# Cross attention and mixture of experts: the last unit's sums, residuals, router rows and first keys in another order

## The reference, cut to what matters

```python
# attention, on the layer-normed x; keys and values are both ctx
qn, kn = l2norm(q), l2norm(k)                     # over the 64 channels of a head
sm = softmax(5.0 * einsum('bhdq,bhdk->bhqk', qn, kn), axis=-1)
x = x + einsum('bhqk,bhdk->bhdq', sm, v)
# experts, on the layer-normed new x: 2048 tokens, 4 experts, capacity 512 each
logits = tokens @ Wg + bg                         # 2048 x 4
top_vals, top_idx = top_k(logits, 2);  probs = softmax of these two
for i in range(4):
    p, idx = top_k(where(i in top_idx, probs[:, i], -inf), 512)
    out[idx] += gelu(tokens[idx] @ W1[i]) @ W2[i] * p
x = x + out
```

## Time and profile before

| | us |
|---|---|
| three runs | 598.73, 602.92, 599.44 |
| median | 599.44 |
| the profiled execution, its time | 601.62 |
| its span, first to last instruction | 599.8 |

### The profile page before, as it was taken

One profiled execution on the slowest core, in us unless ns is written; L12 is line 12 of the kernel. 1 busy time (PEld: TensorE's weight loads), 2 busy tenths in 40 slices (PEclk: granted clock), 3 DMA queues, 4 the chain that ended last, 5 costly groups with the idle time before them and its releaser, 6 DMA issues.

```text
span 599.8 us, 8893 instructions
## 1 busy us (share of the span) xinstructions
PE 569.5 (95%) x2936; PEld 405.8 (68%) x2936; DVE 341.8 (57%) x682; ACT 292.6 (49%) x451; POOL 183.0 (31%) x146
## 2 busy tenths in 40 slices
PE   8999999999998558999999999999999999999994
PEld 4445555545544325888888888888888888888883
DVE  5779999999978683534345434346434346334212
ACT  3989888788884323333234343234343243343310
POOL 8456565565633425000401500401500401500002
PEclk9999999999997859999999999999999999999998
DMA  5524433433223134322622532622632612632001
GB/s 156 194 73 124 143 106 110 141 109 104 90 89 113 65 105 140 120 91 71 184 98 89 198 135 70 203 77 87 209 123 76 203 70 94 198 128 71 0 1 70
DMA packets 49005, 67.91 MB, mean 113 GB/s; under 512 B 10961, under 2 KB 27473, under 8 KB 48977
## 3 DMA queue, kind: packets, MB, share of 16 engines
q1 hardware_dynamic: 45136, 54.97, 28.1%
q0 software_dynamic: 3840, 12.59, 6.2%
HBM read 54.77 MB, written 12.64 MB: 112 GB/s over the span
## 4 chain that ended last, share of the span: by engine, by line
PE 86%; DVE 6%; issue 3%; POOL 2%; ACT 1%; DMA 1%; DVEq 0%; POOLq 0%; ACTq 0%
PE two L1532 29%; PE four L1562 10%; PE four L1561 10%; PE four L1559 10%; PE two L1355 9%; PE four L1345 7%; PE two L1370 2%; PE bank_t L1390 2%; PE bank_m L1317 1%; PE bank_t L1324 1%; PE four L1397 1%; DVE junk L1118 1%; PE bank_t L1382 1%; PE bank_m L1332 1%; DMA x_got<-x2n_dram,idx_all 1%
## 5 line engine op out<-in xcount | busy, mean ns | idle before, releaser
L816 ACT ACTIVATE h_f<-two 128x512 f32<-128x512 f32 x64 | 38.3, 598 | 224.2 <-PE two L1532 224.2
L1285 DVE TENSOR_TENSOR h_lo<-h_f,h_hi 128x512 fp32r<-128x512 f32 x64 | 44.1, 689 | 120.2 <-ACT h_hi L817 120.2
L1532 PE MATMUL two<-xt_hi,w_hi 128*128 (+1 forms) x256 | 101.3, 396 | 0.7 <-ACT xt_hi L805 0.7
L1532 PE MATMUL two<-xt_hi,w_lo 128*128 (+1 forms) x256 | 99.9, 390 | 0.0
L1562 PE MATMUL four<-w_hi,h_lo 128*128 128x512 f32 x256 | 99.6, 389 | 0.0
L1559 PE MATMUL four<-w_hi,h_hi 128*128 128x512 f32 x256 | 99.6, 389 | 0.0
L1561 PE MATMUL four<-w_lo,h_hi 128*128 128x512 f32 x256 | 99.6, 389 | 0.0
L1532 PE MATMUL two<-xt_lo,w_hi 128*128 (+1 forms) x256 | 99.2, 389 | 0.0
L706 ACT ACTIVATE prob<-four,rnorm 128x512 f32<-128x512 f32 x128 | 77.9, 705 | 18.2 <-POOL rnorm L518 15.0
L1255 DVE TENSOR_TENSOR w_lo<-raw,w_hi 128x2048 fp32r<-128x2048 f32 x30 | 68.7, 2291 | 23.3 <-ACT w_hi L739 23.3
L518 POOL TENSOR_TENSOR rnorm<-ss_max,power 128x8 f32<-128x8 f32 x32 | 59.2, 1851 | 43.0 <-DVE ss_max L869 28.0
(11 more groups left out here) (187 smaller groups left out, 759.2 us busy)
## 6 DMA issues: line engine op xcount, KB each, us to landing
raw<-in_L_ffn_W SPq DMA_DIRECT2D x64, 512.0 KB, 4.3
x_all<-in_x SPq DMA_DIRECT2D x16, 256.0 KB, 2.7
c_sb<-in_ctx SPq DMA_DIRECT2D x16, 256.0 KB, 3.1
out<-x_all SPq DMA_DIRECT2D x16, 256.0 KB, 2.3
x2n_dram<-x2n SPq DMA_DIRECT2D x16, 256.0 KB, 3.0
p_inv<-inv_dram SPq DMA_DIRECT2D x30, 128.0 KB, 2.8
few<-p_sum SPq DMA_DIRECT2D x60, 2.0 KB, 1.8
cst<-in_consts SPq DMA_DIRECT2D x1, 423.5 KB, 4.9
```

What stands on the lines that cost most here:

```text
L1285: nc.vector.tensor_tensor(h_lo[m % 2][:, :], h_f[m % 2][:, :], h_hi[m % 2][:, :].bitcast(F32), ALU.subtract).then_inc(h_split, 1)
L1532: return nc.tensor.matmul(z[:, :], w_part[c][:, w], x_k, start=start, stop=stop)
```

## The change

In the last unit VectorE makes half sums 0 first. TensorE's sums are done in two parts, each as soon as its half sums are there (`last_sums`), ahead of the weighted values, and the router rows of unit 12 go behind the weighted values. The residual of unit 14 moves from GpSimd to VectorE, behind `invert_sums`. The router rows of 14 go to `bank_m` as before, those of 15 to a tile of their own in SBUF (`x2n_last`), so that the transposes of 14 and 15 can both stand ahead of their products. The first keys move from the middle of unit 15 to behind `normalize_x2` of 15; the first count of round 0 goes behind the last keys. TensorE transposes the first keys behind all router products; the idle products are spread otherwise (12, 3, 2, 2 in place of 6, 3, 3, 10).

```diff
-            def residual(u):                       # on GpSimd
...
-            residual((UNITS // 2 - 1, 0))
             finish((UNITS // 2 - 1, 0))
             finish((UNITS // 2 - 1, 1))
             pool.wait_ge(x2n_done, UNITS)
             for q in range(2):
                 first_low(0, q)
-            pool.wait_ge(key_done, 2)
+            pool.wait_ge(late_keys, 1)
...
             take_x2t((UNITS // 2 - 2, 1))          # ScalarE
+            take_x2t((UNITS // 2 - 1, 0), bank_m)
+            take_x2t((UNITS // 2 - 1, 1), rows=x2n_last)
             act.wait_ge(key_set, 1)
             nc.scalar.activation(key_w[:, 0:EARLY, :, :], key[:, 0:EARLY, :].unsqueeze(3)
                                  .broadcast_to([P, EARLY, E, WAYS]), ACT.Copy).then_inc(key_done, 1)
-            take_x2t((UNITS // 2 - 1, 0), bank_m)
-            take_x2t((UNITS // 2 - 1, 1))
...
-                if behind > 2:                     # VectorE, unit
+                if behind > 2 and ahead:
                     normalize_x2(before(before(before(u))), behind > 4)
-                if not ahead:
-                    residual(before(before(u)))
-                    statistics_x2(before(before(u)))
...
                 for h in range(2):
                     half_sums(u, 0, h, behind > 0)
+                if not ahead:
+                    normalize_x2(before(before(before(u))), True)
+                    residual(before(before(u)))
                 if behind:
                     invert_few(before(u))
...
-                if not ahead:
-                    normalize_x2(before(before(u)), True)
                 for h in range(2):
                     half_sums(u, 1, h, behind > 0)
-                if not ahead:
-                    dve.wait_ge(logit_done, EARLY)
-                    keys_of(0, EARLY)
-                if behind > 2:
+                if behind > 2 and ahead:
                     take_logits(before(before(before(u))))
-                if behind > 1 and ahead:
-                    residual(before(before(u)))
+                if behind > 1:
+                    if ahead:
+                        residual(before(before(u)))
                     statistics_x2(before(before(u)))
...
             invert_sums(end)                       # VectorE, tail
+            residual(before(end))
+            residual(end, 1)
+            normalize_x2(before(before(end)), True)
+            take_logits(before(before(before(end))))
             statistics_x2(before(end))
-            residual(end, 1)
+            statistics_x2(end)
             normalize_x2(before(end), True)
             take_logits(before(before(end)))
-            statistics_x2(end)
             normalize_x2(end, True)
+            dve.wait_ge(logit_done, EARLY)
+            keys_of(0, EARLY)
             take_logits(before(end), bank_m)
+            take_logits(end)
             early = EARLY * P
+            dve.wait_ge(logit_done, UNITS)
+            keys_of(EARLY, UNITS)
+            dve.wait_ge(key_set, 2)
+            nc.vector.tensor_copy(key_w[:, EARLY:, :, :], ...).then_inc(late_keys, 1)
             dve.wait_ge(key_t, 1)
             dve.wait_ge(thr_done, 1)
             link(nc.vector.tensor_scalar(junk[:, 0:early - SIGNS], ...))
             dve.wait_ge(signs_done, 1)
             put(nc.vector.scalar_tensor_tensor(rest0[:, :], count0[:, :], -2.0, excess[:, :], ALU.mult, ALU.add))
-            take_logits(end)
-            dve.wait_ge(logit_done, UNITS)
-            keys_of(EARLY, UNITS)
-            dve.wait_ge(key_set, 2)
-            nc.vector.tensor_copy(key_w[:, EARLY:, :, :], ...).then_inc(key_done, 1)
...
+            def last_sums(u, n):                   # TensorE
+
+                for h in range(2):
+                    pe.wait_ge(halves_done[h], 2 * number(u) + n + 1)
+                pe.wait_ge(sum_taken, number(u))
+                for h in range(2):
+                    last = nc.tensor.matmul(o_ps[1][DH * h:DH * (h + 1), :], cst[:, C_ONES:C_ONES + DH],
+                                            half_sum[h][n][:, :], start=(n == 0), stop=(n == 1))
+                if n:
+                    last.then_inc(sums_ready, 1)
...
-                if behind > 2:                     # TensorE, unit
-                    router_logits(before(before(before(u))))
-                if not ahead:
-                    sums(u, behind, ahead)
-                weighted_values(u, 2)
-                weighted_values(u, 3)
-                if ahead:
-                    sums(u, behind, ahead)
+                    if behind > 2:
+                        router_logits(before(before(before(u))))
+                    weighted_values(u, 2)
+                    weighted_values(u, 3)
+                    sums(u, behind)
+                else:
+                    last_sums(u, 0)
+                    last_sums(u, 1)
+                    weighted_values(u, 2)
+                    weighted_values(u, 3)
+                    router_logits(before(before(before(u))))
...
+            idle_products(12)                      # TensorE, tail
             pe.wait_ge(logit_done, UNITS - 3)
             transpose_x2(before(before(end)))
+            idle_products(3)
             router_logits(before(before(end)))
-            pe.wait_ge(exp_done, TT * UNITS)
-            transpose_keys(0, EARLY, 1)
-            idle_products(6)
             transpose_x2(before(end), bank_m)
-            idle_products(3)
-            router_logits(before(end), bank_m)
             pe.wait_ge(logit_done, UNITS - 2)
             transpose_x2(end)
-            idle_products(3)
-            router_logits(end)
-            idle_products(10)
-            transpose_keys(EARLY, UNITS, 2)
+            router_logits(before(end), bank_m)
+            router_logits(end, rows=x2n_last)
+            idle_products(2)
+            pe.wait_ge(exp_done, TT * UNITS)
+            transpose_keys(0, EARLY, key_done)
+            idle_products(2)
+            transpose_keys(EARLY, UNITS, late_keys)
```

More of the change, by code:

```diff
@@ L314, in xattn_moe_kernel @@
         key_done = sem("key_done")
+        late_keys = sem("late_keys")
         key_t = sem("key_t")
@@ L545, in key_remainders @@
                 pool.wait_ge(k_split, n + 1)
-            def residual(u):
[L549 to L556, removed]
             def finish(u):
@@ L726, in take_sums, with take_x2t @@
                 nc.scalar.activation(p_sum[:, :], o_ps[1][:, :], ACT.Copy).then_inc(sum_taken, 1)
-            def take_x2t(u, bank=bank_t):
+            def take_x2t(u, bank=bank_t, rows=x2n_t):
                 act.wait_ge(x2t_ready, number(u) + 1)
-                nc.scalar.activation(x2n_t[:, :, :], bank[:, :].rearrange("p (k t) -> p k t", k=KD),
+                nc.scalar.activation(rows[:, :, :], bank[:, :].rearrange("p (k t) -> p k t", k=KD),
                                      ACT.Copy).then_inc(x2t_taken, 1)
@@ L1084, in _ @@
             invert_sums(end)
+            residual(before(end))
+            residual(end, 1)
+            normalize_x2(before(before(end)), True)
+            take_logits(before(before(before(end))))
             statistics_x2(before(end))
-            residual(end, 1)
+            statistics_x2(end)
             normalize_x2(before(end), True)
             take_logits(before(before(end)))
-            statistics_x2(end)
             normalize_x2(end, True)
+            dve.wait_ge(logit_done, EARLY)
+            keys_of(0, EARLY)
             take_logits(before(end), bank_m)
+            take_logits(end)
             early = EARLY * P
+            dve.wait_ge(logit_done, UNITS)
+            keys_of(EARLY, UNITS)
+            dve.wait_ge(key_set, 2)
+            nc.vector.tensor_copy(key_w[:, EARLY:, :, :], key[:, EARLY:, :].unsqueeze(3)
+                                  .broadcast_to([P, UNITS - EARLY, E, WAYS])).then_inc(late_keys, 1)
             dve.wait_ge(key_t, 1)
@@ L1357, in weighted_values, with sums @@
                 last.then_inc(pv_done, 1)
-            def sums(u, behind, ahead):
+            def sums(u, behind):
                 for h in range(2):
@@ L1366, in sums @@
                     for h in range(2):
-                        if ahead:
-                            row = QUAD * (2 * n + h)
-                            last = nc.tensor.matmul(o_ps[1][row:row + QUAD, :], cst[:, C_ONES:C_ONES + QUAD],
-                                                    half_sum[h][n][:, :], start=True, stop=True,
-                                                    tile_position=(0, row))
-                        else:
-                            last = nc.tensor.matmul(o_ps[1][DH * h:DH * (h + 1), :], cst[:, C_ONES:C_ONES + DH],
-                                                    half_sum[h][n][:, :], start=(n == 0), stop=(n == 1))
-                last.then_inc(sums_ready, 1)
+                        row = QUAD * (2 * n + h)
+                        last = nc.tensor.matmul(o_ps[1][row:row + QUAD, :], cst[:, C_ONES:C_ONES + QUAD],
```

(11 more changed lines are left out.)

4 lines of the change are left out of this document (1 added, 3 removed).

## The result

The changed kernel takes 602.54 us (median of 20 runs, 602.14 to 603.64), the kernel before 599.27 us (median of 20). The ratio is 1.0052, 95% interval 1.0042 to 1.0063: slower by 3.1 us, half a percent. Single executions far outside the rest (one of 1449.97 us among these 20 of the kernel before) are left out of all ratios. That is within 1%, as forecast, but above the range that was given (597.2 to 600.5) and on the other side of no change.

The account below looks back on a forecast made before the run. TensorE's expert stage fills most of the span; only 177 to 204 us can move. 2.2 us gained in unit 15, 1.4 lost to the moved residual, with newly exposed first keys: net 0.65 off median 599.44, 598.8 us, range 597.2 to 600.5.

Parts of the forecast that it names:

- What bounds the kernel: Whole kernel: only 177 to 204 us, 27 us or 4.5% of the span, can move; the rounds behind shift whole.
- Unit 15: Unit 15: earlier half sums and split sums let VectorE's inversion start at about 184.2, not 186.39; 2.2 us gained.
- The tail on VectorE: VectorE behind the inversion: the residual moved there takes 1.4 of the 2.2 us gained; `normalize_x2` of 15 ends at 194.7.
- T: The end of `normalize_x2` of 15 on VectorE: forecast 194.7 us, before 195.49.
- D: Length from the start of unit 14's sums to the start of the second part of round 0's count.
- From T to the rounds: Behind `normalize_x2` of 15: keys, transposes and count; the last-keys path alone gives 3.1 us, the whole 0.65.
- The first keys' way: Ahead of the rounds: ScalarE's copy, twelve transposes, signs, four transposes, no longer hidden; second part of count starts at 203.3.
- The clock: TensorE's tail: half clock when the twelve key transposes begin, returning during them or the idle products behind.
- the clock holds: Rival, chance 0.20: full clock through the key transposes, rounds begin 1.4 to 1.9 us earlier, 597.7 us.
- The base of the sum: Final sum: 0.65 us off the profiled span 599.8, then the same step off the runs' median 599.44, giving 598.8.
- slower: Rival, chance 0.08: twelve idle products at half clock delay the rows and logits of 13; 601.8 us.

Follow-up runs that it names:

- the second profile: The changed kernel, unaltered, timed and profiled again beside the kernel before: 602.8 us, ratio 1.0051; the profiled execution's own time was 602.32.
- GpSimd behind the last keys: Changed kernel with GpSimd's first two parts of `w_lo` waiting until the last keys are copied: 600.89 us, ratio 1.0020 to the kernel before.

## Why the prediction was wrong, step by step

**What bounds the kernel.** Right: only 177 to 204 us changed, and what follows shifted as a whole.

**Unit 15.** The sum put the inversion at 184.2, 8.3 us behind the start of unit 14's sums; it was 8.15 in three of the five profiles with the changed order of unit 15 and no keys in it (9.5 and 9.2 in the other two, the changed kernel's first and the one with the residual on GpSimd, where the last small transfer took 3.1 and 2.8 us to land in place of 1.8). The size was right, its reason was not: the 2.2 us were booked to the half sums and sums. The sums alone give nothing, since before the first keys ended on VectorE at 186.33, just as the sums did (183.73 + 2.63 = 186.36). Only with the keys moved away as well does the inversion move, and they have to be made somewhere.

**The tail on VectorE.** T was put 18.8 us behind that zero and was 18.3 in the second profile. The residual moved to VectorE was booked as 1.4 us lost of the gain. Left on GpSimd, it makes VectorE wait 2.3 us, so the move gains about 1 us in D. The step looked at the queue that got the work and priced at nothing the wait for the engine that lost it.

**From T to the rounds, the step that failed first.** "VectorE meanwhile makes the first keys, some 2.75 us: they end at T + 2.8." They ended at T + 4.84. The price of 2.75 was read where GpSimd is idle; the new place is the very moment at which `x2n_done` lets GpSimd start on `w_lo`. The prediction wrote that "GpSimd's first parts of `w_lo` wait for the last keys as before" and gave them no price. That was misread. In the kernel before, too, only the third part waits for the last keys, and the first two start as soon as `normalize_x2` of 15 is done, where VectorE was then idle for 2.9 us:

```profile
195.57 2.49 POOL L580 TENSOR_TENSOR w_lo<-raw,w_hi 128x512 fp32r<-128x512 f32 x2 [0.66 <-DVE x2n L957]
```

The trace of before held the warning, at its start, which wasn't read (timeline of the kernel before, two conversions of one shape, the second beside an operation of GpSimd):

```profile
14.49 0.22 DVE L976 CAST ones_b<-cst 128x128 bf16<-128x128 f32 x1
14.52 1.34 POOL L543 TENSOR_TENSOR k_lo<-c_sb,k_hi 128x512 fp32r<-128x512 f32 x1 [0.56 <-DVE wide_q L898]
14.62 1.32 DVE L977 CAST block_b<-cst 128x128 bf16<-128x128 f32 x1
```

The Trainium skill, page "SBUF — State Buffer", section "Who interferes with whom", says that VectorE and GpSimd share a pair of ports, that a VectorE instruction with two SBUF inputs or in a two-port mode competes for it with a GpSimd instruction that reads SBUF, and that the later one waits for the whole of the other. The rows agree: two-input operations and a conversion take about as long as GpSimd's operation beside them (1.26 to 1.34). Weighed against this change, the rule names a loss of two GpSimd operations less what the two comparisons cost anyway, 2.7 - 0.55 = 2.1 us by the rows, which is what was measured in the keys (T + 4.84 less T + 2.69 with GpSimd out of the way is 2.15). Of it 1.9 reached the end.

**The first keys' way** (copy, twelve transposes, signs, four transposes): right in its links. The forecast for the whole, 203.3, is D = 27.4. The kernel with GpSimd out of the way has 27.21, at half clock in the transposes as expected. That it is so near is partly luck: T came 0.5 us earlier than forecast, and the way from T to the count took 8.9 us and not 8.6, 0.3 of it the new collision in the count.

**The clock.** It was at half when the transposes began, in all the kernels with the change's idle products, as forecast. Its return was forecast for the transposes or the idle products behind them. So it was in the changed kernel's second profile (0.59 from 202 to 204 us, 1.00 from 204 to 206; the last four transposes took 0.60), but not in the first (0.50 from 194 to 210 us, the four took 1.06). The rival "the clock holds" needs more idle products, and is then worth 1.2 us in D (1.4 to 1.9 forecast).

**The base of the sum, the second failure.** The gain of 0.65 was taken from D = 28.05 of a single execution and then subtracted from the median. The prediction noted that this execution lay 2.18 us above the median and carried the distance through as if it were the profiler's. It lay inside the stretch, with the clock at half in two places: D is 25.2 and 26.5 in the two others. Against those a forecast D of 27.4 is a loss of about 1 to 2 us, and a loss of 1.2 us remains with the collision removed (ratio 1.0020). So 1.9 of the 3.1 us is shown by moving GpSimd's operations; that the other 1.2 is the base is an account that fits the lengths, and no run tests it by itself. The rival "slower" had the size (601.8) but the wrong place: logits of 13 were on time.

## What to carry to other kernels

When work moves, read its price where it will run: list what the other engines do in that window, and look in the trace for two instances of the same operation and shape with different durations. When a profile's own time is above the median by more than the gain that is forecast (here 2.2 us against 0.65), find out first whether the surplus lies in the stretch that is to be changed; a second profile of the same kernel settles it. A wait that is shortened on one engine only helps if the engine next in line had nothing else ahead of it in its queue.

## What the runs showed of the hardware that was not expected

- VectorE operations of 0.2 to 0.35 us take 1.16 to 1.43 us beside a GpSimd `tensor_tensor` of about 1.3 us: two-input ones of 128x192, `tensor_scalar` with one 128x48 input, a conversion of 128x128. Two-input ones of 128x1 took 0.47 to 0.54 in place of 0.16. The counting operation, which reads PSUM, did not suffer: 0.75 us for 128x512 with GpSimd at work on `w_lo` ("GpSimd behind the last keys", 201.37) and 0.75 with GpSimd idle (the changed kernel, 204.40).
- TensorE's clock in one and the same program fell to 0.50 in two stretches, one or none of 177 to 196 us in three executions, whose times were 601.62, 600.25 and 598.24. With seven idle products in the two gaps ahead of the fall it came 5 us later in the profiled execution, and the median stayed where it was. Twelve fp32 transposes of 128x128 are 1.50 us at full and 2.79 at half clock.
- The last of four transfers of 2 KB landed after 1.8 us in most executions, after 3.1 in the first of the changed kernel and after 2.8 in that with the residual on GpSimd. In these two the issue of the store that follows it in the queue took 1.48 and 1.17 us, and 0.58 in all others. Which of the two delays causes the other, or what causes both, isn't shown.
